# Four moved waits and a quantizer unit split in two, in a kernel of a ternary feed-forward layer and a top-2 expert layer on one core

## What is computed

```python
w = weights[subjects]                                  # per sample, 64 x 64
y = einsum('bct,bcd->bdt', x, w)                       # mixes channels
h = silu(gate(y)) * up(y)                              # 512 -> 2048, ternary weights
x = x + rms_norm(h) @ ternary_quant(w_proj).T          # 2048 -> 512
H = x @ W.T + (x @ A[idx].T) @ B[idx].T * s[idx]       # linear layer with an adapter
logits = (H @ router_w.T + router_b).reshape(T, O, 8)  # a router of 8 per output element
c = top-2 softmax weights, summed over the O elements  # T x 8
x = x + einsum('te,teo->to', c, einsum('th,eoh->teo', H, expert_w) + expert_b)
```

## Time and profile before

| what | value |
|---|---|
| time, median of 3 runs | 2304.49 us (2302.49 to 2305.18) |
| time of the profiled execution | 2306.22 us |
| its span, first to last instruction | 2304.5 us |
| mean granted clock of TensorE in it | 0.981 |
| PE busy | 2207.9 us, 96% of the span |
| DVE busy | 1625.1 us, 71% |
| ACT busy | 1053.1 us, 46% |
| POOL busy | 59.3 us, 3% |

### The profile page before, as it was taken

The page is one execution under the profiler, slowest core; times in us unless marked ns, Lnnn a source line. Parts: engine busy times, 40 slices in busy tenths (PEclk is TensorE's granted clock), DMA queues, the critical chain, the costliest instruction groups (busy, mean ns, idle before and its releaser), DMA issues.

```text
span 2304.5 us, 28740 instructions
## 1 busy us (share of the span) xinstructions
PE 2207.9 (96%) x9817; PEld 1814.9 (79%) x9817; DVE 1625.1 (71%) x2119; ACT 1053.1 (46%) x1493; POOL 59.3 (3%) x55
## 2 busy tenths in 40 slices
PE   7999999696969889999999999999999999999999
PEld 5777888585858678788888888888788888888887
DVE  8985444343433234568999999999898888888883
ACT  7754333232322223367877878778332222222221
POOL 0000001010010100200000000000000000000000
PEclk9999999898989989999999999999999999999999
DMA  6314213231322312532121212116322222222220
GB/s 206 106 41 140 76 37 116 46 116 46 116 64 76 100 40 55 187 110 87 69 77 68 82 68 82 68 68 241 110 96 82 77 96 82 78 96 77 83 82 23
DMA packets 157908, 205.66 MB, mean 89 GB/s; under 512 B 63330, under 2 KB 96674, under 8 KB 155682
## 3 DMA queue, kind: packets, MB, share of 16 engines
q1 hardware_dynamic: 114578, 149.95, 19.6%
q10 hardware_dynamic: 43152, 55.06, 7.3%
q0 software_dynamic: 128, 0.07, 0.0%
HBM read 136.35 MB, written 68.68 MB: 89 GB/s over the span
## 4 chain that ended last, share of the span: by engine, by line
PE 76%; issue 14%; DVE 3%; POOL 2%; ACT 1%; SPq 1%; DMA 1%; POOLq 0%; ACTq 0%; DVEq 0%
PE slot L1650 10%; PE ex_bank L1825 9%; PE ex_bank L1827 9%; PE ex_bank L1826 9%; PE high_bank L1792 5%; PE high_bank L1794 5%; PE high_bank L1796 5%; PE pj L1663 5%; PE low_bank L1792 4%; PE low_bank L1796 4%; PE low_bank L1794 4%; PE slot L1712 3%; POOL diff_work L708 2%; PE slot L1619 1%; SPq L511 1%
## 5 line engine op out<-in xcount | busy, mean ns | idle before, releaser
L1650 PE MATMUL slot<-y_hi,wgu 128*128 128x512 f32 x1024 | 402.0, 393 | 1.1 <-DVE q_scale L1168 0.5
L1650 PE MATMUL slot<-y_lo,wgu 128*128 128x512 f32 x1024 | 399.4, 390 | 0.0
L1825 PE MATMUL ex_bank<-ew_hi,hb 128*128 128x512 f32 x992 | 387.3, 390 | 3.5 <-ACT ex_bank L1098 3.5
L1826 PE MATMUL ex_bank<-ew_hi,hb 128*128 128x512 f32 x992 | 386.8, 390 | 0.0
L1827 PE MATMUL ex_bank<-ew_lo,hb 128*128 128x512 f32 x992 | 386.8, 390 | 0.0
L1098 ACT ACTIVATE ex_bank<-eb_sb 128x512 f32<-128x512 f32 x248 | 149.1, 602 | 456.5 <-DVE acc L1557 395.4
L1507 DVE SCALAR_TENSOR_TENSOR lead_in<-code_in,wts 128x1024 bf16<-128x1024 bf16 x256 | 311.8, 1218 | 1.8 <-DVE code_in L1434 0.4
L1663 PE MATMUL pj<-wpj,hid_hi 128*128 128x512 f32 x484 | 194.7, 402 | 72.5 <-DVE hid_lo L1232 72.5
L1650 PEld LDWEIGHTS slot<-y_hi,wgu 128*128 128x128 f32 x1024 | 192.3, 188 | 44.6 <-DVE q_scale L1168 2.8
L1650 PEld LDWEIGHTS slot<-y_lo,wgu 128*128 128x128 f32 x1024 | 192.4, 188 | 39.7
L1825 PEld LDWEIGHTS ex_bank<-ew_hi,hb 128*128 128x128 f32 x992 | 186.7, 188 | 42.6 <-ACT ex_bank L1098 3.9
(11 more groups left out here) (169 smaller groups left out, 3560.6 us busy)
## 6 DMA issues: line engine op xcount, KB each, us to landing
hb<-h_scratch SPq DMA_DIRECT2D x34, 512.0 KB, 3.5
code_scratch<-half_code SPq DMA_DIRECT2D x32, 512.0 KB, 2.6
half_in<-code_scratch SPq DMA_DIRECT2D x32, 512.0 KB, 3.3
hb<-h_scratch ACTq DMA_DIRECT2D x30, 512.0 KB, 3.6
h_scratch<-ht ACTq DMA_DIRECT2D x48, 256.0 KB, 2.9
q_raw<-in_w_ffn SPq DMA_DIRECT2D x21, 512.0 KB, 3.4
x_scratch<-x_res ACTq DMA_DIRECT2D x8, 1024.0 KB, 4.4
lead_scratch<-lead SPq DMA_DIRECT2D x32, 256.0 KB, 2.0
```

The source lines that it names most:

```text
L1650: last = mm(slot[s % 2][:, g, :], wgu[:, c, r * P:(r + 1) * P], y[:, c, :], start=(c == 0 and v == 0), stop=(c == DC - 1 and v == 1))
L1825: mm(ex[e][:, :], hb[:, u, c, 0, :], ew_hi[:, e, c, :], start=False, stop=False, skip_group_check=True)
L1826: mm(ex[e][:, :], hb[:, u, c, 1, :], ew_hi[:, e, c, :], start=False, stop=False, skip_group_check=True)
```

## The change

Five things are changed; the multiplications on PE and their order are not.

1. Small tiles move to a region of their own at the front of the on-chip memory (1,280 bytes per partition with a filler), so other tiles get other addresses.
2. In SP's loop `rows_for_turning` moves from behind the differences to ahead of them, and the load of `x_mix` from the front to the end.
3. `turned` stands after steps 8 and 9 instead of 9 and 10, on ACT and DVE.
4. In stage 3 ACT makes the last router tile's signs and codes after all 8 seeds of tile 1 instead of after 5 of them (EP is 7), and DVE joins them amid tile 2 instead of ahead of it.
5. On DVE the two low halves of block 0's `mix` stand amid the second quantizer unit, ahead of its `quant_sign`, instead of behind it.

```diff
         ident = sb("ident", [P, P], F32)
+        early_small = ExitStack()
+        group_mean = sb("group_mean", [P, P], BF16, early_small)
+        ones_col = sb("ones_col", [P, 1], F32, early_small)
...
+        early_small.close()
+        late_small = ExitStack()
+        step_col = sb("step_col", [P, 4], F32, late_small)
+        c_ring = sb("c_ring", [P, 4, E], F32, late_small)
+        late_small.close()
+        small_end = sb("small_end", [P, 320], F32)
...
                 sp.wait_ge(drained, mixed)
-                sp.dma_start(x_mix[:, :, :], one(XB, i)).then_inc(xmix_in, 16)
                 gather_mix(i, mixw, mixw_in)
+                sp.wait_ge(x1t_ready, sp.snap(i * 2 - 6))
+                rows_for_turning(i - 2)
                 piece = one(RWC, i - 4)
...
                     sp.wait_ge(diff_out, sp.snap(i * (16 * EP) + 16 * (e + 1 - 4 * EP)))
-                sp.wait_ge(x1t_ready, sp.snap(i * 2 - 6))
-                rows_for_turning(i - 2)
+                sp.dma_start(x_mix[:, :, :], one(XB, i)).then_inc(xmix_in, 16)
...
-                    if j in (9, 10):
-                        turned(i - 1, j - 9)
+                    if j in (8, 9):
+                        turned(i - 1, j - 8)
...
-                        if isinstance(m, int) and u == 1 and e == 4:
+                        if isinstance(m, int) and u == 1 and e == EP:
                             sign(NT - 1, 1, L[:, 0, EP - 1, :], (NT + 1) * KT)
                             place(NT - 1)
...
             quant(0)
-            quant(1)
+            quant_scale(1)
+            quant_gap(1)
             mix(0)
+            quant_sign(1)
...
-            def tile(n, k, pair):
+            def tile(n, k, pair, between=None):
 
 
                 for e in range(E):
                     expert(n, e, k, pair)
+                    if e == 4 and between is not None:
+                        between()
...
-            join(NT - 1)
-            for n in range(2, 4):
-                tile(n, n, n // 2)
+            tile(2, 2, 1, lambda: join(NT - 1))
+            tile(3, 3, 1)
```

More of the change, by code:

```diff
@@ L185, in build @@
         ident = sb("ident", [P, P], F32)
+        early_small = ExitStack()
+        group_mean = sb("group_mean", [P, P], BF16, early_small)
+        ones_col = sb("ones_col", [P, 1], F32, early_small)
+        var = sb("var", [P, SUB], F32, early_small)
+        inv = sb("inv", [P, SUB], F32, early_small)
+        minus_half = sb("minus_half", [P, SUB], F32, early_small)
+        subject_i = sb("subject_i", [1, NB_SAMPLES], I32, early_small)
+        idx_i = sb("idx_i", [P, NB_SAMPLES], I32, early_small)
+        adapter_i = sb("adapter_i", [P, 1], I32, early_small)
+        adapter_f = sb("adapter_f", [P, 1], F32, early_small)
+        scal_sb = sb("scal_sb", [P, 1], F32, early_small)
+        lmask = sb("lmask", [P, NB_SAMPLES], F32, early_small)
+        early_small.close()
[4 more added lines that the diff above has]
+        small_end = sb("small_end", [P, 320], F32)
         pa = ExitStack()
@@ L207, in build @@
         hid1 = sb("hid1", [P, RING, BLK], F32, pa)
-        group_mean = sb("group_mean", [P, P], BF16, pa)
         py = ExitStack()
@@ L225, in build @@
         sumsq = sb("sumsq", [P, BLK], F32, pa)
[L226 to L235, removed]
         pq = ExitStack()
@@ L275, in build @@
         wts = sb("wts", [P, 2, 2, D], F32, p2)
-        step_col = sb("step_col", [P, 4], F32, p2)
         lead_in = sb("lead_in", [P, 2, D], F32, p2)
@@ L281, in build @@
         digits = sb("digits", [P, 2, D], F32, p2)
-        c_ring = sb("c_ring", [P, 4, E], F32, p2)
         p3 = ExitStack()
```

## The result

The changed kernel takes **2215.84 us** (median of 4 runs, 2214.54 to 2215.89); the kernel before, on the same chip, 2304.02 us (4 runs, 2302.49 to 2305.18). The ratio is 0.9616, 95% interval 0.96 to 0.9633: 88 us faster. The forecast was 2216.9 us. Its profiled execution has a span of 2214.1 us.

A forecast was written before the change was run, and what follows sets the result against it. PE, busy 96%, bounds the kernel; only its waits and clock losses can be won. Terms -81.6, -2.5, -5.1 and +1.6 sum to -87.6 us, from a span of 2304.5 to 2216.9 us; range 2213 to 2226.

The forecast's parts named there:

- SP's new order: Blocks 3 to 6: rows issued ahead of the differences remove their whole excess over block 2, -81.6 us.
- x_mix hidden: SP's queue: `x_mix`, issued at 419, lands at 424, 25 us before block 4, costing nothing; rival of waiting 1 in 100.
- The turning one step earlier: Blocks 2 to 7: six PE waits for `x1t_lo` go, -2.5 us; bounds 0 and 3.1, the latter with 0.1 restart each.
- POOL in DVE's way: Rival: beside the turning, one POOL difference in each of four blocks delays PE, 5 us, giving 2222 us; 5 in 100.
- The addresses: Tiles' new places: same instructions on the same sizes run, so 0 us.
- The experts: PE's 3.46 us wait for a seed and 1.6 us of lost clock go, -5.1 us; bounds 3.5 and 5.5.
- The load of `hb`: Rival in the experts: tile 3's load behind the signs comes late, tile 3 stands, up to 2222 us; 5 in 100.
- The first block: DVE's three operations come later, delaying the product and second `gu`, +1.6 us; bounds 0 and 2.2.
- The clock's fall there: Rival in the first block: clock falls behind PE's idle stretch of 3.1 us, 1.6 us more, 2218.5 us; 20 in 100.

The follow-up runs named there:

- the signs as before: Changed kernel with change 4 undone (signs and codes after 5 seeds, join ahead of tile 2): 2222.36 us.
- the turning where it was: Changed kernel with change 3 undone, `turned` after steps 9 and 10 again: 2219.83 us.
- POOL kept short: Changed kernel with POOL subtracting only 8 of 512 columns of each difference: 2212.52 us.
- the matrices last: Changed kernel with `x_mix` first in SP's loop again and the mixing matrices (`gather_mix`) behind the differences: 2214.96 us.
- `x1t` moved: Changed kernel with `x1t` and the small tiles behind it 32 bytes further, the matrices where they were: 2219.18 us.

## Why the forecast was right, and where not

The changed kernel took 2215.84 us; the sum said 2216.9, and -87.6 us against -90.4 in the spans. The large term was right in mechanism and size, and several small ones were off in both directions.

- *SP's new order, -81.6.* Right. SP alone gave 79.3 us in blocks 3 to 6; the missing 2.3 belongs to the rival on POOL, below.
- *x_mix hidden.* Right: issued at 419.00 as worked out, landing 5 us later, 24 us ahead of the mix at 448.26.
- *The turning one step earlier, -2.5.* Right in mechanism, under-sized: 0.74 a block in the clean block 2, thus 4.4 in six, beyond the bound of 3.1 too. The sum took the waits as listed, 0.42 a block. A wait is listed from the end of the matmul before it, 0.39 us after its start, while without it the next would have started after 0.23; these 0.16 us were left out, and the 0.1 of restart stood in the bound alone. In the blocks with POOL, 1.7 us of it were given back.
- *POOL in DVE's way.* The rival that was given 5 in 100 came true, in the terms in which it was priced: three blocks, 1.3 us each, 3.9 us. The forecast looked for it in block 3 up to the gap of before, where DVE had slack, and took "PE lost nothing" for a sign, though it had itself moved POOL's work to where DVE has none. It should have had more than 5 in 100. The trace of before held the sign on DVE itself, in block 5, where `hid_lo` took 1.80 us instead of 0.69:

```profile
630.97 1.29 POOL L708 TENSOR_TENSOR diff_work<-diff_work,diff_base 128x512 f32<-128x512 f32 x1 [8.36 <-DMA diff_work<-in_rwT]
631.00 1.80 DVE L1232 TENSOR_TENSOR hid_lo<-hid,hid_hi 128x512 fp32r<-128x512 f32 x1 [0.70 <-ACT hid_hi L789]
```

- *The addresses, 0.* Wrong, and this is the step that failed: "the same instructions on the same sizes run" was taken for the same time. They gave 2.7 us in the medians when changed alone, and 3.9 by the pace of 576 matmuls. The trace of before held the sign: matmuls of one shape and type had a mean of 396 ns in the linear layer and 390 in `gu` with `y_lo`.
- *The experts, -5.1.* Right, a little under-sized. The gap is 3.8 us when measured by itself, where the sum had the listed 3.5, and the fall of the clock that the kernel before had behind it is the other 1.6: 5.4 us. That fall does not come each time, as the run with the signs as before shows. The load of `hb` was not late.
- *The first block, +1.6.* Right: +1.5 from the first mix to the second `gu`, both in the changed kernel and with the change alone.
- *The clock's fall there, rival at 20 in 100.* In the changed kernel's profile it did not come where it was looked for: it came one product earlier, and the slower `gu` shortened the gap to 1.49 us. In five other profiles (the turning where it was, POOL kept short, the matrices last, `x1t` moved, the fifth change alone) the gap was 3.0 us, and in each the clock fell behind it, for 1.5 us. So it is the likelier case once the first `gu` has its full clock, and 20 in 100 was too low.

Together the misses nearly cancel: -3.9 for the addresses, -1.9 for the turning, -0.3 for the experts and -0.8 for a first mix that happened to start earlier, against +3.9 for POOL, make -3.0, and the span was 2.8 us below the sum. That the time came within 1.1 us of the forecast is luck as far as these terms go: an effect that was put at nothing and a rival that was given 5 in 100 are of the same size and of opposite sign.

## What to carry to other kernels

When a queue's order is changed, also ask which of the other engines' work moves with it: POOL's subtraction, moved with SP's queue, met VectorE in a tight stretch, and a meeting cost VectorE up to 1.1 us where its own instruction came second. Where such work can't be moved, shorter instructions make a meeting cheaper (up to 0.54 us with halves of 0.74). Count a listed wait of TensorE at about 0.3 us more than the list gives, as its neighbours' starts show. And lay out the operands of matmuls at the same remainder mod 64 bytes: on 3,072 matmuls of 512 columns that is worth 19 us against 32 bytes apart.

## What the runs showed of the hardware

- A matmul of 128 by 512 takes 0.233 us where its operands stand 32 bytes apart mod 64, and 0.227 where they stand at the same remainder; shifting both changes nothing (2215.79 against 2215.84 us). Other distances weren't tried.
- VectorE's addition of 512 columns, begun 0.07 us behind a GpSimd subtraction of 1.30 us, took 1.78 us instead of 0.69; begun 0.15 us ahead of one, 0.69, and the subtraction took 1.68. The product `hid`, one of whose two inputs lies in PSUM, where matmuls write, kept its 0.69 beside a subtraction (begun at 495.33 and 495.43 us in the changed kernel), and the subtraction its 1.29.
- The granted clock behind an idle stretch is not settled by its length. All fourteen profiles have a stretch of 2.15 us at the start; the clock fell at its end or within 1 us behind it in six of them, the changed kernel among them, and in eight, the kernel before among them, it did not. Behind 3.0 us at the start it fell in all five profiles that had it. Behind 3.5 us in the experts it fell in four of five (0.58 over 4 us in the kernel before), and not with the signs as before (1.00 behind 3.49 us). The Trainium skill, page "TensorE: Matmul & The Clock Gate", section "Why this matters for your kernels", asks for no idle gaps of the order of these 3.0 and 3.5 us between bursts of matmuls; the runs agree, with nine falls in ten cases, but the falls behind 2.15 us show that shorter gaps aren't safe either. Where PE was the limit a fall cost 1.1 to 1.6 us. What decides between the two cases stays open.
